# Row statistics made where the rows are finished, one square root per router head, and rows kept in on-chip memory between two stages of a four-layer block

## Chip, core and metric

The kernel runs on one core of a Trainium2 chip. The metric is the time of one execution on the device in microseconds (us), the median of the runs shown. All data is float32. TensorE is called PE, VectorE DVE, ScalarE ACT, GpSimd POOL; SyncE (SP) issues the DMA transfers that this change touches.

## The reference, cut to what matters

```
x = x + attention(layernorm(x))          # x is 2048 tokens by 512
x = x + ffn(layernorm(x))
x = x + rwkv(layernorm(x))               # recurrence over the 2048 tokens
x = x + ffn(layernorm(x))
layernorm(x) = (x - mean(x)) / sqrt(var(x) + 1e-5)      # over the 512 of a row
ffn(h): scores = sigmoid(h @ gate_w); 2 of 4 groups, 6 of 32 experts of each token
        sum of 6 weighted silu(h @ w_gate) * (h @ w_up) @ w_down
        + silu(h @ sw_gate) * (h @ sw_up) @ sw_down      # shared expert, 704 wide
```

## The kernel before

Tokens are 16 tiles of 128 rows, four tiles to a block, so there are four blocks (`NB = 4`, `BT = 4`). The stages run one after another: projections, attention, attention output (`stage_attn_out`), router with the shared expert (`stage_router`), experts (`stage_experts`), the recurrence (`stage_rwkv`), and router and experts again. Each stage is a block of programs, one for each engine, that are ordered among each other only by semaphores; a stage begins when all engines have ended the one before. Within an engine the order is the order written. Where precision asks for it a matrix is split into a high part (made by ACT) and a low part (made by DVE), and three products are added.

**Attention output.** For each of 16 tiles PE turns the heads, ACT makes the high part, DVE the low part (`low_heads`, L848), PE multiplies, and DVE adds the product to the residual rows `resid` (`add_rows`, L853). `resid` holds all 16 tiles in on-chip memory; the blocks lie in it in the order `ORDER = [2, 3, 0, 1]` (`place_of`).

**The router's head.** This is everything up to the first product of the shared expert, `up(0)` (L1613). In the second router SP first loads `resid` from DRAM, where the recurrence stored it (L1110). SP then loads the gate weights, the shared expert's up weights in two halves (`wup`, L1116) and its down weights (`wdown`, L1117 and L1119), then stores the normalized rows `xn` block by block (L1126). `xn` has room for two blocks: block 2 can be normalized only when block 0's store has landed (`xn_stored[0]`), block 3 when block 1's has.
- DVE: `statistics(0, 2, 1)` makes `bn_stats` (L1335) and `bn_aggr` (L1339) of eight tiles, adds epsilon, waits for ACT's square root, makes the reciprocal root in five short steps, and normalizes eight tiles (L144). Then `statistics(2, NB, 2)` does the same for the other eight, and `low_shared(0)` makes the low part of half the up weights.
- ACT: `root(0)`, the copies of blocks 0 and 1 after PE has turned them (`copy_block`, L1210, four copies a block), `copy_logits(0)` (L1216), `high_shared(0)` (L1248), `root(1)`, `copy_logits(1)`, `high_shared(1)`, `copy_block(2)`, `copy_block(3)`, `copy_logits(2)`, and the high part of block 2 (L1263). DVE makes its low part (L1365), and PE starts `up(0)`. The high part of the down weights (L1268) comes after that.
- PE: turns block 0, multiplies it with the gate, then block 1, then turns blocks 2 and 3 and multiplies both.

**The recurrence.** It runs over 16 units `n = 4 * b + c` (block `b`, quarter `c` of the channels). In each, PE makes three projections (24 products, L2375) and the output product of unit `n - 3` (eight products, L2387). DVE runs in this order: `sums(n-1)` (two scans, L2267 and L2269), `advance_peak(n)` (a scan, L2259, and a difference, L2262), `quotients(n-3)` (L2288), at `c == 3` `add_out(b-1)` (four additions of the output to `x_add`, L2302), `divide(n-2)` (three operations and a reciprocal, L2275 to L2280), `finish_mix` (L2254), at `c == 1` the row statistics of block `b + 2` (`stats`), at `c == 3` its normalization (`normalize`). POOL's four products of a unit (L2125, L2110, L2114, L2116) are released by `division_begun`, which DVE raises ahead of its reciprocal. After the last unit POOL does `fraction_top` of units 14 and 15 in one go. SP stores the sums of each block to DRAM (`time_mixed`, L2097), waits until the stores have landed, and loads `x_add` for the next block (L2101).

Of the kernel before, what the change touches and what calls it, by code (L numbers as in the profile page):

```python
# [31 lines left out]
BT = 4  # L32
# [65 lines left out]
class Norm:  # L98
# [5 lines left out]
    def __init__(self, k, name, scope, n_blocks=NB):  # L104
        nc = k.nc
        self.stats = scope.enter_context(nc.sbuf_tensor(f"{name}_stats", [P, n_blocks, BT, 6], F32))
# [708 lines left out]
def stage_attn_out(k, w, ident, heads, resid):  # L815

    nc = k.nc
    with ExitStack() as s:
# [10 lines left out]
        product, added = k.sem("c_product"), k.sem("c_added")  # L829

        k.clear_past()
        with nc.Block() as block:
# [12 lines left out]
            def _(v):  # L845
# [119 lines left out]
def stage_router(k, name, ident, resid, source, gate_w, shared_up, shared_down, xn_rows, acc_rows, disp, first, weights):  # L965
# [4 lines left out]
    with ExitStack() as s:  # L970
# [63 lines left out]
        norm = Norm(k, f"{name}_norm", s)  # L1034
# [41 lines left out]
        resid_loaded = [sem(f"resid_loaded{b}") for b in range(NB)]  # L1076
# [27 lines left out]
        with nc.Block() as block:  # L1104
            @block.sync
            def _(sp):
                if source is not None:
                    resid_in = rows(source)
                    for b in range(NB):
                        sp.dma_start(resid[:, place_of(b):place_of(b) + BT, :], resid_in[:, b * BT:(b + 1) * BT, :]).then_inc(resid_loaded[b], 16)  # L1110
                        if b == 0:
                            sp.dma_start(wg[:], gate_w).then_inc(gate_loaded, 16)
                else:
                    sp.dma_start(wg[:], gate_w).then_inc(gate_loaded, 16)
                for i in range(2):
                    sp.dma_start(wup[i][:], shared_up[:, :, UP_HALF[i]]).then_inc(up_loaded[i], 16)  # L1116
                sp.dma_start(wdown[:, 0:FULL, :], shared_down[0:FULL * P, :].rearrange("(c p) d -> p c d", p=P)).then_inc(down_loaded, 16)  # L1117
                for half in (slice(0, TAIL), slice(TAIL, P)):
                    sp.dma_start(wdown[half, FULL, :], shared_down[FULL * P:SM, :]).then_inc(down_loaded, 16)  # L1119
# [4 lines left out]
                for b in range(NB):  # L1124
                    sp.wait_ge(normed, (b + 1) * BT)
                    sp.dma_start(xn_out[:, b * BT:(b + 1) * BT, :], xn[:, b % 2 * BT:(b % 2 + 1) * BT, :]).then_inc(xn_stored[b % 2], 16)  # L1126
                for i in range(2):
# [76 lines left out]
            def _(act):  # L1204
# [36 lines left out]
                def root(n):  # L1241
                    span = slice(n * NB // 2, (n + 1) * NB // 2)
                    act.wait_ge(norm.var_ready, n + 1)
                    act.activation(norm.std[:, span, :], norm.var[:, span, :], ACT.Sqrt).then_inc(norm.std_ready, 1)

# [4 lines left out]
                root(0)  # L1250
# [4 lines left out]
                root(1)  # L1255
# [38 lines left out]
            def _(v):  # L1294
# [34 lines left out]
                def statistics(first, last, roots):  # L1329
                    span = slice(first, last)  # L1330
                    for b in range(first, last):
                        if source is not None:
                            v.wait_ge(resid_loaded[b], 16)
                        for t in range(BT):
                            chain.step(v.bn_stats(norm.stats[:, b, t, :], resid[:, place_of(b) + t, :]))  # L1335
                    chain.wait()
                    for b in range(first, last):
                        for t in range(BT):
                            chain.step(v.bn_aggr(norm.mean_var[:, b, t, :], norm.stats[:, b, t, :]))  # L1339
# [1185 lines left out]
```

## Time and profile before

| what | value |
|---|---|
| median of 3 runs | 3247.44 us (3246.61 to 3250.93) |
| profiled execution, its own time | 3245.94 us |
| its span | 3244.2 us |
| PE busy / DVE / ACT / POOL | 94% / 64% / 49% / 27% |
| attention output | ends at 849.94 us |
| first router and experts | 850.2 to about 1890 us |
| recurrence | about 1897 to 2182.47 us |
| second router and experts | 2185.05 us to the end |

A row of the time line has the start in us, the length in us, the engine, the line, the operation, what is written and read, the count of merged instructions, and in brackets how long the engine had idled and what released it. PEld is PE's loading of weights. In groups merged from several instructions the length reaches from the first start to the last end.

### The profile page before, as it was taken

Reading aid. Unit: us, or ns where it says so; the run is one execution under the profiler, and the core shown is the slowest. Engines: PE = TensorE matmul, PEld = TensorE weight load, DVE = VectorE, ACT = ScalarE, POOL = GpSimd, SP = SyncE. Lnnn points to the kernel's source line nnn. Section 1 sums busy time; section 2 is a strip of 40 time slices with the busy share of each in tenths; the row PEclk is TensorE's granted clock in tenths of the full one; section 3 lists DMA queues with packets and bytes.
Section 4 is the critical chain, followed back from the end, with each engine's and each line's share of the span. In section 5 each row is a group of like instructions: output and inputs, shape, how many; then the busy total and the mean of one; then the engine's idle time right before and its main releaser. Section 6 shows DMA issues by size and latency. Waiting matters only on the chain. (4 is left out here: it accounts for less than half of the span.)

```text
span 3244.2 us, 62788 instructions
## 1 busy us (share of the span) xinstructions
PE 3060.3 (94%) x15682; PEld 2414.2 (74%) x15683; DVE 2078.7 (64%) x3887; ACT 1591.8 (49%) x2096; POOL 867.9 (27%) x777
## 2 busy tenths in 40 slices
PE   8979999999799999999999969977999999999998
PEld 6745555555678799999999944436788999999997
DVE  5266666663686566666666659987765666666665
ACT  3224544444321366665665657634124666566665
POOL 0011000110011243333333313341113343333333
PEclk9969999999999999999999989998999999999999
DMA  6331111130300477776777540114016777777664
GB/s 188 113 77 41 41 40 40 40 105 1 125 30 29 129 180 170 177 176 165 183 180 174 115 147 0 52 52 176 30 48 174 187 186 177 171 181 170 169 153 77
DMA packets 142697, 378.72 MB, mean 117 GB/s; under 512 B 22144, under 2 KB 24960, under 8 KB 139008
## 3 DMA queue, kind: packets, MB, share of 16 engines
q1 hardware_dynamic: 88832, 248.20, 24.5%
q0 software_dynamic: 52608, 127.69, 20.8%
q10 hardware_dynamic: 1152, 1.57, 0.2%
q8 instruction: 48, 0.79, 0.1%
q14 instruction: 57, 0.47, 0.0%
HBM read 277.49 MB, written 99.91 MB: 116 GB/s over the span
## 5 line engine op out<-in xcount | busy, mean ns | idle before, releaser
L1905 DVE TENSOR_TENSOR first_lo<-first_raw,first_hi x230 | 557.8, 2425 | 95.3 <-ACT first_hi L1850 95.0
L1850 ACT ACTIVATE first_hi<-first_raw x230 | 465.4, 2023 | 23.0 <-DVE first_lo L1905 7.6
L607 ACT ACTIVATE b_probs<-b_p_cols 128x1024 f32<-128x1024 f32 (+1 forms) x320 | 269.2, 893 | 300.2 <-PE b_p_cols L739 299.1
L1898 DVE TENSOR_TENSOR g_hidden<-g_gate,g_p_up 128x352 f32<-128x352 f32 x232 | 120.9, 521 | 450.8 <-PE g_p_up L1965 447.1
L1861 ACT ACTIVATE g_y<-g_p_y,first_rows_in 128x512 f32<-128x512 f32 x232 | 160.0, 690 | 345.6 <-PE g_p_y L1981 345.5
L1963 PE MATMUL g_p_gate<-first_hi,first_rows_hi 128*128 (+1 forms) x928 | 319.1, 344 | 4.6 <-DVEq L1921 4.4
L638 DVE TENSOR_REDUCE b_part_max<-b_p_ring 128x1 f32<-128x512 f32 x384 | 246.4, 686 | 117.4 <-PE b_p_ring L724 115.2
L1802 POOL DMA_INDIRECT out_dram<-g_y,first_ids_out x116 | 186.4, 1607 | 441.7 <-ACT g_y L1861 327.8
L1802 POOL DMA_INDIRECT mixed_rows<-g_y,first_ids_out x116 | 183.9, 1585 | 443.4 <-ACT g_y L1861 331.1
L1964 PE MATMUL g_p_gate<-first_lo,first_rows_hi 128*128 (+1 forms) x928 | 300.5, 324 | 0.0
L1965 PE MATMUL g_p_gate<-first_hi,first_rows_lo 128*128 (+1 forms) x928 | 299.4, 323 | 0.0
L1965 PE MATMUL g_p_up<-first_hi,first_rows_lo 128*128 (+1 forms) x928 | 298.0, 321 | 0.0
L1963 PE MATMUL g_p_up<-first_hi,first_rows_hi 128*128 (+1 forms) x928 | 297.9, 321 | 0.0
L1964 PE MATMUL g_p_up<-first_lo,first_rows_hi 128*128 (+1 forms) x928 | 297.8, 321 | 0.0
L1979 PE MATMUL g_p_y<-first_hi,g_hidden_hi 128*128 (+2 forms) x696 | 275.3, 395 | 7.4 <-issue 5.6
L1980 PE MATMUL g_p_y<-first_lo,g_hidden_hi 128*128 (+2 forms) x696 | 274.5, 394 | 0.0
L1981 PE MATMUL g_p_y<-first_hi,g_hidden_lo 128*128 (+2 forms) x696 | 274.3, 394 | 0.0
L755 PE MATMUL b_p_out<-b_probs,b_v_pair 128*64 128x512 f32 (+3 forms) x1280 | 270.3, 543 | 0.0
L1791 POOL DMA_INDIRECT first_rows_in<-xn_rows,first_ids_in x232 | 241.6, 1042 | 71.7 <-issue 70.8
L724 PE MATMUL b_p_ring<-b_k_stack,b_q_stack 96*128 96x512 f32 (+3 forms) x640 | 220.4, 424 | 24.9 <-ACT b_shift_t L593 9.8
L1836 ACT ACTIVATE g_gate<-g_p_gate 128x352 f32<-128x352 f32 x232 | 108.1, 466 | 248.1 <-issue 188.1
L724 PEld LDWEIGHTS b_p_ring<-b_k_stack,b_q_stack 96*128 96x128 f32 x640 | 112.8, 197 | 149.9 <-issue 43.0
(364 smaller groups left out, 6473.8 us busy)
## 6 DMA issues: line engine op xcount, KB each, us to landing
first_raw<-in_expert_weights_dram SPq DMA_DIRECT2D x248, 544.0 KB, 8.0
qk_hi<-a_hi SPq DMA_DIRECT2D x32, 256.0 KB, 2.6
qk_lo<-a_lo SPq DMA_DIRECT2D x32, 256.0 KB, 2.9
xn_rows<-f_xn SPq DMA_DIRECT2D x8, 1024.0 KB, 8.3
b_q_stack<-qk_hi SPq DMA_DIRECT2D x28, 256.0 KB
b_k_stack<-qk_hi SPq DMA_DIRECT2D x28, 256.0 KB
first_raw<-in_expert_weights_dram SPq DMA_DIRECT2D x2, 2176.0 KB, 8.6
resid<-in_x_dram SPq DMA_DIRECT2D x4, 1024.0 KB, 10.8
```

Of the source, the lines that this page charges most:

```text
L607: act.activation(probs[:, q, :, 0:w], p_cols[:, m % NCOL, :, 0:w], ACT.Exp, scale=SCALE).then_inc(probs_ready, 1)
L724: pe.matmul(p_ring[:, ring, 0:w], q_stack[i][h][0:NPART, t * P:(t + 1) * P], k_stack[i][h][0:NPART, c * BW:c * BW + w], start=True, stop=T ...
L755: mm = pe.matmul(p_out[h * HV:(h + 1) * HV, d:BW], v_pair[i][:, kt, h, :], probs[:, m % NPROB, h, 0:BW - d], start=(kt == 0), stop=(m in l ...
L1802: pool.indirect_dma_start(out=acc_rows, out_offset=bass.IndirectOffsetOnAxis(ap=ids_out[:, i:i + 1].bitcast(U32), axis=0), in_=y[:, n, :], ...
L1850: act.activation(hi[:, bass.ds(place, PIECE)], raw[:, bass.ds(source, PIECE)], ACT.Copy).then_inc(split_hi_ready, 1)
L1905: v.tensor_tensor(lo[:, bass.ds(place, PIECE)], raw[:, bass.ds(source, PIECE)], hi[:, bass.ds(place, PIECE)].bitcast(F32), ALU.subtract).t ...
L1963: pe.matmul(p_g[:, i, 0:M], rows_hi[:, i, c, :], hi[:, columns], start=(c == 0), stop=False)
L1964: pe.matmul(p_g[:, i, 0:M], rows_hi[:, i, c, :], lo[:, columns], start=False, stop=False)
L1965: m = pe.matmul(p_g[:, i, 0:M], rows_lo[:, i, c, :], hi[:, columns], start=False, stop=(c == KD - 1))
L1979: pe.matmul(p_y[:, i, :], hidden_hi[0:z, i, c, :], hi[0:z, columns], start=(c == 0), stop=False)
L1980: pe.matmul(p_y[:, i, :], hidden_hi[0:z, i, c, :], lo[0:z, columns], start=False, stop=False)
L1981: m = pe.matmul(p_y[:, i, :], hidden_lo[0:z, i, c, :], hi[0:z, columns], start=False, stop=(c == MC - 1))
```

## The change

It has four parts.
1. `bn_stats` of a tile is made where the tile is finished: in the attention output after each `add_rows`; in the recurrence in four places, the last block's after each of its four additions, blocks 0, 1 and 2 at `n = 14, 15, 16` after `divide`. The results lie in one tensor, `row_stats`, that outlives the stages. Both routers read it.
2. The router's head aggregates all 16 tiles, takes one square root, and makes one reciprocal root for all.
3. The recurrence writes blocks 2 and 3 of its result straight to where the second router has `resid`. Blocks 0 and 1 still go through DRAM (`half_rows`) and are loaded to that place while the recurrence runs, after the third block's projections. The router loads nothing of `resid`.
4. SP loads the down weights behind the stores of `xn` blocks 0 and 1. In the recurrence `stats` and `normalize` stand ahead of `divide`, and POOL's last `fraction_top` waits for `division_begun` of its own unit.

```diff
 # stage_attn_out, DVE
                     v.tensor_tensor(resid[:, place, :], p_mm[:, t % 2, :], resid[:, place, :], ALU.add).then_inc(added, 1)
+                    v.wait_ge(added, t + 1)
+                    v.bn_stats(row_stats[:, t // BT, t % BT, :], resid[:, place, :]).then_inc(stats_ready, 1)
 # stage_router, SP
-                if source is not None:
-                    resid_in = rows(source)
-                    for b in range(NB):
-                        sp.dma_start(resid[:, place_of(b):place_of(b) + BT, :], ...).then_inc(resid_loaded[b], 16)
...
-                sp.dma_start(wdown[:, 0:FULL, :], ...).then_inc(down_loaded, 16)
-                for half in (slice(0, TAIL), slice(TAIL, P)):
-                    sp.dma_start(wdown[half, FULL, :], shared_down[FULL * P:SM, :]).then_inc(down_loaded, 16)
...
                 for b in range(NB):
                     sp.wait_ge(normed, (b + 1) * BT)
                     sp.dma_start(xn_out[:, b * BT:(b + 1) * BT, :], ...).then_inc(xn_stored[b % 2], 16)
+                    if b == 1:
+                        sp.dma_start(wdown[:, 0:FULL, :], ...).then_inc(down_loaded, 16)
+                        for half in (slice(0, TAIL), slice(TAIL, P)):
+                            sp.dma_start(wdown[half, FULL, :], ...).then_inc(down_loaded, 16)
 # stage_router, ACT
-                root(0)
+                act.wait_ge(norm.var_ready, 1)
+                act.activation(norm.std[:], norm.var[:], ACT.Sqrt).then_inc(norm.std_ready, 1)
                 copy_block(0)
                 copy_block(1)
                 copy_logits(0)
                 high_shared(0)
-                root(1)
                 copy_logits(1)
 # stage_router, DVE
-                statistics(0, 2, 1)
                 for b in range(NB):
-                    if b == 2:
-                        statistics(2, NB, 2)
+                    for t in range(BT):
+                        chain.step(v.bn_aggr(norm.mean_var[:, b, t, :], norm.stats[:, b, t, :]))
+                chain.wait()
+                v.tensor_scalar(norm.var[:], norm.mean_var[:, :, :, 1], EPS, None, ALU.add).then_inc(norm.var_ready, 1)
+                v.wait_ge(norm.std_ready, 1)
+...
+                for b in range(NB):
 # stage_rwkv, SP
-                for b in range(NB):
+                for b in range(NB - 1):
                     for t in range(BT):
                         sp.wait_ge(out_added, b * BT + t + 1)
-                        sp.dma_start(out_tiles[:, b * BT + t, :], x_add[:, t, :]).then_inc(out_stored[t], 16)
+                        if b < STORED:
+                            sp.dma_start(half_tiles[:, b * BT + t, :], x_add[:, t, :]).then_inc(out_stored[t], 16)
...
+                    if b == STORED - 1:
+                        sp.wait_ge(product, (NB - 1) * KD * 3)
+                        sp.wait_ge(mixed_ready, 3 * NB)
+                        for half in range(STORED):
+                            sp.dma_start(resid[:, place_of(half):place_of(half) + BT, :], half_tiles[...]).then_inc(resid_loaded, 16)
+                sp.wait_ge(resid_loaded, 16 * STORED)
 # stage_rwkv, POOL
-                pool.wait_ge(division_begun, UNITS - 1)
-                fraction_top(UNITS - 2)
-                fraction_top(UNITS - 1)
+                for n in range(UNITS - 2, UNITS):
+                    pool.wait_ge(division_begun, n + 1)
+                    fraction_top(n)
 # stage_rwkv, DVE
-                        v.tensor_tensor(x_add[:, t, :], p_out[:, t, :], x_add[:, t, :], ALU.add).then_inc(out_added, 1)
+                        into = x_add[:, t, :] if b < STORED else resid[:, place_of(b) + t, :]
+                        v.tensor_tensor(into, p_out[:, t, :], x_add[:, t, :], ALU.add).then_inc(out_added, 1)
+                        if b == NB - 1:
+                            v.wait_ge(out_added, b * BT + t + 1)
+                            v.bn_stats(row_stats[:, b, t, :], resid[:, place_of(b) + t, :]).then_inc(row_stats_ready, 1)
...
+                def row_statistics(b):
+                    if b < STORED:
+                        v.wait_ge(resid_loaded, 16 * STORED)
+                    for t in range(BT):
+                        v.bn_stats(row_stats[:, b, t, :], resid[:, place_of(b) + t, :]).then_inc(row_stats_ready, 1)
...
                     if c == 3 and 1 <= b < NB:
                         add_out(b - 1)
+                    if n < UNITS and b + 2 < NB and c == 1:
+                        stats(b + 2)
+                    if n < UNITS and b + 2 < NB and c == 3:
+                        normalize(b + 2)
                     if 2 <= n < UNITS + 2:
                         divide(n - 2)
+                    if UNITS - 2 <= n <= UNITS:
+                        row_statistics(n - (UNITS - 2))
                     if n < UNITS:
...
-                        if b + 2 < NB and c == 1:
-                            stats(b + 2)
-                        if b + 2 < NB and c == 3:
-                            normalize(b + 2)
```

## Rows read from the trace of the kernel before

**Rows 1.** Page, busy time by engine; busy time of the last expert stage.
```profile
PE 3060.3 (94%) x15682; PEld 2414.2 (74%) x15683; DVE 2078.7 (64%) x3887; ACT 1591.8 (49%) x2096; POOL 867.9 (27%) x777
...
2460.00:3244.00 784.00, 769.98 (x4591) 716.87 (x4588) 486.08 (x689) 466.20 (x577) 304.21 (x230) 0.99 0.69 164
```
**Rows 2.** Time line, end of the attention output.
```profile
841.18 0.69 DVE L848 TENSOR_TENSOR c_heads_lo<-c_p_turn,c_heads_hi 128x512 fp32r<-128x512 f32 x1 [0.38 <-ACT c_heads_hi L839]
...
842.90 0.59 PEld L868 LDWEIGHTS c_p_turn<-ident,heads 128*128 128x128 f32 x4
...
849.25 0.69 DVE L853 TENSOR_TENSOR resid<-c_p_mm,resid 128x512 f32<-128x512 f32 x1 [2.03 <-PE c_p_mm L881]
```
**Rows 3.** Time line, head of the first router.
```profile
850.22 1.28 ACT L1244 ACT_TABLE_LOAD   x1 [5.86 <-PEq L832]
850.26 4.84 DVE L1335 BATCH_NORM_STATS2 f_norm_stats<-resid 128x6 f32<-128x512 f32 x8 [0.32 <-PEq L832]
...
855.13 0.64 DVE L1339 BATCH_NORM_AGGREGATE f_norm_mean_var<-f_norm_stats 128x2 f32<-128x6 f32 x8
...
857.31 3.74 DVE L144 TENSOR_SCALAR f_xn<-resid,f_norm_mean_var,f_norm_rstd 128x512 f32<-128x512 f32 x8
...
871.00 2.38 ACT L1248 ACTIVATE f_wup_hi<-f_wup 128x2560 fp32r<-128x2560 f32 x1
...
874.87 0.60 ACT L1210 ACTIVATE f_xT_f<-f_p_down 128x512 f32<-128x512 f32 x1 [1.49 <-PE f_p_down L1561]
...
880.68 0.60 ACT L1216 ACTIVATE f_logits_t<-f_p_mm 128x512 f32<-128x512 f32 x1 [1.03 <-PE f_p_mm L1569]
...
884.38 0.50 PE L1613 MATMUL f_p_mm<-f_xT_hi,f_wup_hi 128*128 128x512 f32 x1 [1.90 <-DVE f_xT_lo L1365]
```
**Rows 4.** Time line, head of the second router; then its first products by tile.
```profile
2181.78 0.69 DVE L2302 TENSOR_TENSOR r_x_add<-r_p_out,r_x_add 128x512 f32<-128x512 f32 x1 [0.17 <-PE r_p_out L2387]
...
2190.85 2.47 DVE L1335 BATCH_NORM_STATS2 f_norm_stats<-resid 128x6 f32<-128x512 f32 x4 [8.38 <-DMA resid<-time_mixed]
...
2198.41 3.74 DVE L144 TENSOR_SCALAR f_xn<-resid,f_norm_mean_var,f_norm_rstd 128x512 f32<-128x512 f32 x8
...
2228.14 0.71 PE L1613 MATMUL f_p_mm<-f_xT_hi,f_wup_hi 128*128 128x512 f32 x1 [1.90 <-DVE f_xT_lo L1365]
...
L1613 PE MATMUL f_p_mm<-f_xT_hi,f_wup_hi x4: 392/628/713, 2228.1 to 2231.9; 128*128 128x512 f32 x4
```
**Rows 5.** Time line, ACT in the recurrence: a table load and the next root.
```profile
1961.65 1.28 ACT L131 ACT_TABLE_LOAD   x1
1962.94 0.21 ACT L131 ACTIVATE r_norm_std<-r_norm_var 128x4 f32<-128x4 f32 x1
```
**Rows 6.** DMA from 850 to 876 us: rate in 40 slices; stores' time to landing.
```profile
GB/s 0 8 93 126 175 369 411 416 425 403 410 421 390 406 399 381 391 384 381 334 315 309 331 378 394 394 400 397 397 394 394 183 16 0 0 0 0 66 372 388
...
xn_rows<-f_xn SPq DMA_DIRECT2D x4, 1024.0 KB, 8.3
```
**Rows 7.** Time line, the recurrence's middle: three DVE rows, then PE's.
```profile
2005.61 2.29 DVE L2254 TENSOR_TENSOR r_mixed<-r_mixed,r_shifted 128x2048 f32<-128x2048 f32 x1 [2.01 <-ACT r_shifted L2160]
...
2060.74 1.28 DVE L2259 TENSOR_TENSOR_SCAN r_state<-r_w,r_state,r_k 128x512 f32<-128x512 f32 x1 [1.43 <-ACT r_k L2167]
...
2087.36 2.28 DVE L2267 TENSOR_TENSOR_SCAN r_state<-r_kt,r_state 128x512 f32<-128x512 f32 x1
...
2043.54 0.79 PE L2363 MATMUL r_p_turn<-ident,r_xn 128*128 128x128 f32 x4 [5.02 <-DVE r_xn L144]
```
**Rows 8.** Time line, DVE at the recurrence's end.
```profile
2159.58 0.66 DVE L2288 TENSOR_TENSOR r_y<-r_top,r_below 128x512 f32<-128x512 f32 x1
...
2162.58 3.35 DVE L2280 RECIPROCAL r_below<-r_below 128x512 f32<-128x512 f32 x1 [0.16 <-DVE r_below L2278]
...
2166.31 1.68 DVE L2288 TENSOR_TENSOR r_y<-r_top,r_below 128x512 f32<-128x512 f32 x1 [0.38 <-POOL r_top L2116]
...
2175.60 0.69 DVE L2288 TENSOR_TENSOR r_y<-r_top,r_below 128x512 f32<-128x512 f32 x1
```

More of the change, by code:

```diff
@@ L812, in _, with stage_attn_out @@
                 turn_out(NPAIR - 1, NB - 1, bank("out", NSTEP))
-def stage_attn_out(k, w, ident, heads, resid):
+def stage_attn_out(k, w, ident, heads, resid, row_stats):
     nc = k.nc
@@ L962, in __init__, with stage_router @@
         self.release = sb("release", [1, E], I32)
-def stage_router(k, name, ident, resid, source, gate_w, shared_up, shared_down, xn_rows, acc_rows, disp, first, weights):
+def stage_router(k, name, ident, resid, row_stats, gate_w, shared_up, shared_down, xn_rows, acc_rows, disp, first, weights):
     nc = k.nc
@@ L1327, in tile_hots @@
                         v.tensor_scalar(row_hot[:, n % NR, :], iota_p[:], row_of[:, kk, t:t + 1], None, ALU.is_equal).then_inc(row_hot_ready, 1)
[L1329 to L1339, printed above, removed]
-                    chain.wait()
-                    v.tensor_scalar(norm.var[:, span, :], norm.mean_var[:, span, :, 1], EPS, None, ALU.add).then_inc(norm.var_ready, 1)
-                    v.wait_ge(norm.std_ready, roots)
-                    chain.link(v.reciprocal(norm.r0[:, span, :], norm.std[:, span, :]))
-                    chain.link(v.tensor_tensor(norm.half[:, span, :], norm.r0[:, span, :], norm.r0[:, span, :], ALU.mult))
-                    chain.link(v.tensor_tensor(norm.half[:, span, :], norm.half[:, span, :], norm.var[:, span, :], ALU.mult))
-                    chain.link(v.tensor_scalar(norm.half[:, span, :], norm.half[:, span, :], -0.5, 1.5, ALU.mult, ALU.add))
-                    chain.link(v.tensor_tensor(norm.rstd[:, span, :], norm.r0[:, span, :], norm.half[:, span, :], ALU.mult))
                 def low_shared(i):
@@ L2015, with stage_rwkv @@
 NEG = -1e38
-def stage_rwkv(k, ident, x_rows, mixes, decay, first, w_kvr, w_out, out_rows):
+def stage_rwkv(k, ident, x_rows, mixes, decay, first, w_kvr, w_out, half_rows, resid, row_stats):
     nc = k.nc
@@ L2069, in stage_rwkv @@
         x_add_loaded = [sem(f"x_add_loaded{t}") for t in range(BT)]
-        out_stored = [sem(f"out_stored{t}") for t in range(BT)]
-        x_tiles, out_tiles = rows(x_rows), rows(out_rows)
+        out_stored, resid_loaded, row_stats_ready = [sem(f"out_stored{t}") for t in range(BT)], sem("resid_loaded"), sem("row_stats_ready")
+        x_tiles, half_tiles = rows(x_rows), rows(half_rows)
+        STORED = NB // 2
+        assert sorted(ORDER[:STORED]) == list(range(STORED, NB))
         def shifted_of(b, j):
```

59 lines of the change are left out of this document (32 added, 27 removed).

## The prediction

> **What bounds the kernel now.** I read the page's busy times first. PE works 94% of the span, and the long expert stages are PE's alone: 770 of 784 us in the last one [rows 1]. Nothing in this change touches them. So the question is what the stretches cost in which PE waits: the two router heads and the recurrence. I went through these in order of time, engine by engine, and asked at each idle bracket what ended it. The reader is to see a relay in the heads. Statistics on DVE, a root on ACT, normalization, PE's turning, ACT's copies; none of it overlaps, and PE's first shared product comes only at its end. From the last addition of the attention output (849.25 + 0.69 = 849.94) to that product (884.38) it is 34.44 us; in the second head, from 2182.47 (2181.78 + 0.69) to 2228.14, it is 45.67 us [rows 2 to 4].
>
> **First head.** Five things change.
> - The tail of the attention output. DVE waits for PE before each addition (2.03 us before the last one), so 15 of 16 `bn_stats` go into idle time, at 4.84 / 8 = 0.61 us each [rows 2, 3]. Each pushes the next `low_heads` back by about 0.4 us; it ended at 841.87, and PE wanted it at 842.90, so 1.0 us of cover is left 0.6 [rows 2]. Without that cover it would be 0.4 us for each of 14 tiles, 5.6 us. The last `bn_stats` stands alone behind the last addition: +0.7.
> - From stage start (850.22) to the first normalization (857.31) it was 7.1 us. Now: 16 aggregations at 0.08, 1.3; from the last aggregation through the root to the normalization it was 857.31 - 855.77 = 1.54, and with twice the columns 1.6. That is 2.9 us: -4.2 [rows 3].
> - `root(1)` goes. It stood on ACT behind the first up half, so DVE could not normalize block 2 in time, and ACT, done at 873.38, idled 1.49 us until 874.87. With all rows normalized early it finds block 2 turned: -1.5 [rows 3].
> - ACT's eight copies of blocks 2 and 3 took 874.87 to 879.65 because PE turned blocks just ahead of them. At ACT's own pace, 0.5 each, about 4.1: -0.7. The wait of 1.03 ahead of `copy_logits(2)` shrinks to about 0.3, since PE turned block 3 ahead of ACT's last four copies: -0.7 [rows 3].
> Sum: 0.7 - 4.2 - 1.5 - 0.7 - 0.7 = -6.4.
>
> The down weights are needed only after `up(0)` begins, at 884 before and about 878 now, so their later load costs nothing if it lands by then. By order in SP's queue: gate and up weights 2.95 MB, spare rows 0.28, blocks 0 and 1 at 1.05 each, then 1.57 MB of down weights. The rate is about 0.40 MB per us, flowing some 3 us after the stage's start [rows 6]. Block 0's store lands about 10.7 us after that, 13.7 after the start; block 1's 2.6 later; the down weights 3.9 later still, at 20 us, and they are wanted at 27. Block 2 normalized then is turned by about 17, while ACT comes to it at about 19. So the slack of the stores is some 2 us, of the down weights 7.
>
> Is the table of the square root in time? Its load lasts 1.28 us from the stage's start, and the variance is now ready at 1.5 instead of 5.6 us [rows 3], so the cover shrinks to 0.2. The recurrence's rows have the root 0.01 us behind the load [rows 5]: nothing is added. The Trainium skill (ScalarE: Activation LUTs, What ACT_TABLE_LOAD costs) adds a drain of about 1.38 us to each switch of tables. By it the root would be 1.2 us late in each head and the time 2.4 us longer; this trace has no such gap behind the load, so I don't count it.
>
> **Second head.** It keeps the same instructions from its normalization on, so it takes what the first will: 2.9 to the first normalization and, from there, 27.07 - 1.5 - 0.7 - 0.7 = 24.2 to `up(0)`. Ahead of it stand the last `bn_stats` (0.7), about 0.3 for the stage to turn (849.94 to 850.22), and 0.5 because the `bn_stats` of tile 2 delays the addition of tile 3, which came 0.17 us after it was free to. That is 28.6 against 45.67: -17.1 [rows 3, 4]. Most of it is one thing: `resid` went to DRAM and back, DVE sat 8.38 us for it, and the stores of `xn` were queued behind 4.2 MB more [rows 4]. At the start of `up(0)` PE's products were slow (0.63 against 0.39 us) for 3.5 us, some 1.5 us lost; I leave that as it is, and keep -1.5 for the range [rows 4].
>
> **The recurrence, units 3 to 15.** `stats` and `normalize` move ahead of `divide` in three places that matter (units 3, 5, 7). Ahead of `divide` they run while POOL rests. Behind the reciprocal they shielded the scans: a scan took 2.28 us beside POOL and 1.28 without it [rows 7], so each move costs about 1 us, most of it given back by a small step of the normalization that POOL had held up. For: PE's turning no longer waits 5.02 us for the rows of block 3; DVE's wait of 1.43 for the projection two units later goes, and of the wait of 2.01 in unit 5 about 0.7 is won, since `stats` fills it [rows 7]. Together -0.7 in unit 5, +0.3 left of the contention in unit 7, -1.4 in unit 9: -1.8, which PE, busy without a gap from unit 12 to 15, carries to unit 15. I take -1.8; bounds are -5.0 (PE's whole wait) and +3.0 (three contended scans, no wait won).
>
> **Its end.** The 12 `bn_stats` of blocks 0 to 2 are 2.4 us for each of units 14, 15, 16. The first four are free: POOL ends meanwhile and both scans are uncontended. The second four displace two contended scans (they took 3.6 for 2.4): +1.2. The third four push `quotients(14)` from 2166.31 to 2169.5, +3.2 in all. Then POOL's later release pays back: from `quotients(14)` to the last reciprocal it was 5.90 us beside POOL, and without it the same steps took 3.00 (2159.58 to 2162.58), -2.9. Last, POOL's three products now begin with the reciprocal and end 3.65 us later, the reciprocal after 3.39, +0.3 [rows 8]. Together +0.65; with the units before: -1.2. `bn_stats` beside POOL is not in the trace. Its bounds are the reciprocal (3.35 us with POOL working) and a two-input operation (1.68 for 0.69) [rows 8]. It has one input like the reciprocal, so I take no slowing; the other end is +1 in each of three units. The Trainium skill (SBUF — State Buffer, Who interferes with whom) says that a DVE instruction with one input from on-chip memory does not contend with GpSimd. By that rule too the sum stays; by a lock for every instruction it would be 3 us more.
>
> The load of blocks 0 and 1 into `resid` is issued at about 2107 and needs some 7 us for 2.1 MB; DVE asks at about 2138. Hidden; were the cover gone, up to 7 us. Behind SP's two new waits stand only the loads for block 3's addition, wanted 25 us later.
>
> **Sum.** -6.4 - 17.1 - 1.2 = -24.7. The profiled execution took 3245.94 us and would take 3221.2; it stands 1.5 under the median of 3247.44, so I predict 3222.7 for the median.
>
> **Rivals.**
> 1. The stores become the bound. If the down weights share the queues with block 1's store instead of following it, it lands 3.9 us later, block 3 is turned 2 us after ACT wants it, in both heads: +4, 3226.7. For it: 2 us of slack is little. Against: before, landings agreed with the order of issue (8.3 us behind 4.6 MB of loads) [rows 6].
> 2. The recurrence gives back. All 12 `bn_stats` fully on the path (7.3), three contended scans (3.0), no wait won: +10.3 less POOL's 2.9, so +7.4 in place of -1.2: 3231.3. Against: DVE had idle time in units 5 and 9 [rows 7].
> 3. More is won. PE's 5.02 us come through whole (-3.2 more), and PE starts `up(0)` at full clock (-1.5): 3218.0.
> 4. Slower than before. PE rests about 25 us less, and its clock may be granted lower afterwards. The granted clock was 0.99 over the last expert stage [rows 1]; the two expert stages are about 1710 us. From a drop of 1.5% on it eats the whole gain; at 3% the time is 3274. Against: PE already works hundreds of microseconds on end there with no such drop.
> 5. The change does nothing. That needs a head bound by something that stays, such as ACT's copies; but ACT has nothing to copy before the first normalization, 13.4 us into the second head [rows 4].
>
> **How the numbers follow.** Forecast 0.62, rival 1 0.10, rival 2 0.14, rival 3 0.10, rival 4 0.03, rival 5 0.01. The range, 3215 to 3231, reaches from 3 us beyond rival 3 (the sum's many small gains may each be a little larger) to rival 2. A measurement can tell about 0.2% (6.5 us) from no change; so faster has 0.96, same 0.01, slower 0.03.
>
> **What would show it.** In the profile after: the first normalization 2.9 us after each router's start; no `resid` load; no idle of ACT between the second up half and block 2's copies; `up(0)` 27 us after each start; the last two reciprocals about 8.7 us apart, not 9.63. I would be wrong if DVE waits for `xn_stored` at block 2 after 16 us, or if scans beside POOL grow in number.

## The result and the profile after

The changed kernel took 3221.89 us (median of four), the kernel before 3247.03 in the same session. Three of the four executions took 3217.26 to 3223.50 us (median 3220.28) and one, far outside them, 12998.82; the ratio on record, 0.9913 with a 95% interval of 0.9898 to 0.9928, is estimated without it and is not the quotient of the two medians (0.9923). Forecast were 3222.7 and 3215 to 3231. The profiled execution took 3220.28 us, its span is 3218.2.

The page of the kernel after, its first lines and the granted clock in 40 slices, against [rows 1]:

```profile
span 3218.2 us, 62766 instructions
...
PE 3052.7 (95%) x15680; PEld 2411.1 (75%) x15683; DVE 2070.4 (64%) x3875; ACT 1588.8 (49%) x2094; POOL 871.4 (27%) x777
...
PEclk9969999999999999999999979999999999999999
```

PE's busy time is nearly the same (3052.7 us against 3060.3); what went is mostly time in which it waited. The span is 26.0 us shorter. Cut at the last additions and the first products of `up(0)`, from start to end of each stretch:

| stretch | before | after | difference | forecast |
|---|---|---|---|---|
| up to the last addition of the attention output | 849.94 | 846.41 | -3.5 | 0 |
| first head: that addition's end to `up(0)` | 34.44 | 29.22 | -5.2 | -6.4 |
| `up(0)` to the recurrence's first instruction | 1012.9 | 1021.0 | +8.1 | 0 |
| recurrence, to the end of its last addition | 285.2 | 283.2 | -2.0 | -1.2 |
| second head | 45.67 | 28.10 | -17.6 | -17.1 |
| second `up(0)` to the end | 1016.1 | 1010.3 | -5.7 | 0 |

The three changed stretches give -24.8 where -24.7 was forecast. The three others moved by -3.5, +8.1 and -5.7 and nearly cancel. None of this can be put down to the change: the first stretch ends anywhere from 845.57 to 849.60 us in the executions of the experiments, and the last section comes back to the expert stages.

The timeline of the kernel after, first head, against [rows 3]:

```profile
847.42 1.28 ACT L1241 ACT_TABLE_LOAD   x1 [6.57 <-PEq L832]
849.24 0.21 ACT L1241 ACTIVATE f_norm_std<-f_norm_var 128x16 f32<-128x16 f32 x1 [0.53 <-DVE f_norm_var L1327]
850.80 3.87 DVE L144 TENSOR_SCALAR f_xn<-resid,f_norm_mean_var,f_norm_rstd 128x512 f32<-128x512 f32 x8
...
862.35 1.92 DVE L144 TENSOR_SCALAR f_xn<-resid,f_norm_mean_var,f_norm_rstd 128x512 f32<-128x512 f32 x4 [7.69 <-DMA xn_rows<-f_xn]
...
865.01 2.38 ACT L1238 ACTIVATE f_wup_hi<-f_wup 128x2560 fp32r<-128x2560 f32 x1
867.24 0.64 ACT L1205 ACTIVATE f_xT_f<-f_p_down 128x512 f32<-128x512 f32 x1
...
871.93 0.60 ACT L1211 ACTIVATE f_logits_t<-f_p_mm 128x512 f32<-128x512 f32 x1 [0.63 <-PE f_p_mm L1547]
...
875.63 0.79 PE L1591 MATMUL f_p_mm<-f_xT_hi,f_wup_hi 128*128 128x512 f32 x1 [1.90 <-DVE f_xT_lo L1343]
```

The middle part of the relay is gone. There is one root for 16 columns instead of two, normalization begins 3.4 us after the start, and ACT goes from the second up half (865.01) into block 2's copies without a bracket. DVE has a new wait: 7.69 us until block 0's store has landed, at 862.35, 14.9 us after the start. The row alone doesn't say whether it costs anything; experiment e1 is about that.

The second head, against [rows 4]:

```profile
2179.09 0.67 DVE L2290 TENSOR_TENSOR time_mixed<-r_p_out,r_x_add 128x512 f32<-128x512 f32 x1
2180.78 1.28 ACT L1241 ACT_TABLE_LOAD   x1 [30.68 <-PEq L2057]
...
2182.23 0.22 ACT L1241 ACTIVATE f_norm_std<-f_norm_var 128x16 f32<-128x16 f32 x1 [0.16 <-DVE f_norm_var L1327]
2183.64 3.81 DVE L144 TENSOR_SCALAR f_xn<-time_mixed,f_norm_mean_var,f_norm_rstd 128x512 f32<-128x512 f32 x8
2195.60 1.92 DVE L144 TENSOR_SCALAR f_xn<-time_mixed,f_norm_mean_var,f_norm_rstd 128x512 f32<-128x512 f32 x4 [8.15 <-DMA xn_rows<-f_xn]
...
2207.86 0.50 PE L1591 MATMUL f_p_mm<-f_xT_hi,f_wup_hi 128*128 128x512 f32 x1 [1.90 <-DVE f_xT_lo L1343]
```

Normalization comes 2.86 us after the start (13.36 before), `up(0)` 27.08 after it. DVE's wait for block 0's store, 8.15 us here, was 1.65 before. The root begins 0.17 us after the table load's end (2180.78 + 1.28 = 2182.06), released by the variance.

The recurrence: the first scans of units 1 and 15, the third group of row statistics, and the last quotients, against [rows 7, 8]:

```profile
1936.24 1.28 DVE L2246 TENSOR_TENSOR_SCAN r_state<-r_w,r_state,r_k 128x512 f32<-128x512 f32 x1 [3.29 <-ACT r_k L2154]
...
2142.35 1.28 DVE L2246 TENSOR_TENSOR_SCAN r_state<-r_w,r_state,r_k 128x512 f32<-128x512 f32 x1
...
2163.92 2.41 DVE L2299 BATCH_NORM_STATS2 row_stats<-time_mixed 128x6 f32<-128x512 f32 x4
...
2173.15 0.69 DVE L2275 TENSOR_TENSOR r_y<-r_top,r_below 128x512 f32<-128x512 f32 x1 [0.54 <-POOL r_top L2103]
```

Between those scans lie 206.11 us; before it was 207.85 (1937.51 to 2145.36). So the middle gave 1.74. PE's waits for the rows of blocks 2 and 3 (1.88 and 5.02 us before) are gone. From unit 15's scan to `quotients(15)` it is 30.80 against 30.24, +0.56. Two of the signs named ahead can be read here. The last two reciprocals are 8.60 us apart (8.7 forecast, 9.63 before). Scans slowed beside POOL did grow in number among the sums of units 0 to 13, from 13 to 16: one scan each of units 3, 5 and 7 took 2.28 us and not 1.28. The prediction's sum had counted this as the price of the new order, so this sign did not separate right from wrong. The four scans of units 14 and 15 took 1.54 to 2.22 us before and 1.27 after.

### The profile page after: what moved, and what is told of

It reads as the page before. It is cut to its first block and busy times, and to the rows that moved or that the text cites. A ratio compares the mean times of both kernels' runs of the same rounds, so it can differ in the third digit from the quotient of the medians.

```text
span 3218.2 us, 62766 instructions
## 1 busy us (share of the span) xinstructions
PE 3052.7 (95%) x15680; PEld 2411.1 (75%) x15683; DVE 2070.4 (64%) x3875; ACT 1588.8 (49%) x2094; POOL 871.4 (27%) x777
```

## Experiments

Twelve runs in three groups (e0 to e3, e4 to e7, e8 to e11), each group on one chip with its own runs of the kernel before (3247.47, 3249.10 and 3248.39 us). The changed kernel's own median was 3221.89, 3214.74 and 3218.20 us in different groups, so each experiment is read by the stretches of its profiled execution, and the median stands beside them. Ratios are against the kernel before. "Head" is always from the end of the last addition to the start of `up(0)`.

**The yardstick, twice: e0 and e11.** The changed kernel unaltered, in the first and in the third group.

> The changed kernel itself, unaltered, as the yardstick for the others of this group. Expected 3221.9 us (3218 to 3225), 0.991 of the kernel before. In the profile: first normalization 3 us after each router's start, up(0) 27 to 28 us after it.

> The changed kernel once more, unaltered, on the same chip as these three: 3214 to 3222 us; the stretches from each router's start to up(0) as before, 27.1 to 28.6 us; the expert stages differ by up to 10 us from one execution to the next, which is what the medians can't tell apart.

3214.74 us (0.9894, 0.9879 to 0.9909) and 3218.20 us (0.9902, 0.9882 to 0.9921). Heads 29.54 and 28.60 in e0, 29.12 and 29.15 in e11.

**The down weights ahead of the stores: e1.**

```
+                sp.dma_start(wdown ...)            # ahead of the stores
                 for b in range(NB):
                     sp.dma_start(xn_out[b] ...)
-                    if b == 1:
-                        sp.dma_start(wdown ...)
```

> The down weights are issued before the stores of xn again (1.57 MB ahead of block 0's store, some 3.9 us at 0.40 MB per us); everything else is as in the changed kernel. Theory (the stores are the next bound, with 2 us of slack at most): block 0's store lands about 18.7 us after the router's start and not 14.9, DVE's wait for it at block 2 grows from 8 to 12 us, ACT and PE then wait some 2 us for block 2's rows, and up(0) comes 1.5 to 3 us later in each head, together +3 to +6 us against the changed kernel. Rival (the stores are hidden anyway, since ACT has its copies and the up weights to do): 0, with up(0) still 27 to 28 us after the start.

3222.52 us (0.9922, 0.9908 to 0.9935), +7.8 against e0. Heads 32.78 and 34.01: +3.2 and +5.4. The timeline of its second head:

```profile
2187.58 1.91 DVE L144 TENSOR_SCALAR f_xn<-time_mixed,f_norm_mean_var,f_norm_rstd 128x512 f32<-128x512 f32 x4 [12.37 <-DMA xn_rows<-f_xn]
...
2189.55 1.12 PE L1538 MATMUL f_p_down<-ident,f_xn 128*128 128x128 f32 x4 [5.78 <-DVE f_xn L144]
...
2201.55 0.51 PE L1590 MATMUL f_p_mm<-f_xT_hi,f_wup_hi 128*128 128x512 f32 x1 [1.90 <-DVE f_xT_lo L1342]
```

Block 0's store lands 19.0 us after the start, 3.8 later than in e0, and `up(0)` follows it in full; in the first head it lands 3.7 later and `up(0)` comes 3.2 later. In the second head PE rested 5.78 us before block 2 and then turned at the lower clock (1.12 for four, 0.66 in e0): the 1.6 us more of this head. The transfer was not hidden. With the rest of the change in place, the later load of the down weights is worth about 8 us, and the slack of 2 us that I gave the stores is 0.5 in the first head and none in the second.

**The round trip through DRAM again: e2.**

```
+                        sp.dma_start(half_tiles[b, t], resid[place_of(b) + t])    # recurrence, blocks 2 and 3
+                for b in range(NB):                                               # router, SP
+                    sp.dma_start(resid[b] <- half_rows[b]).then_inc(again_loaded[b], 16)
+                    v.wait_ge(again_loaded[b], 16)                                # router, DVE, ahead of block b
```

> The recurrence stores all four blocks of its output to DRAM again, waits for the last stores before it ends, and the second router loads all 4.2 MB back and waits for each block ahead of its normalization; the row statistics stay where the changed kernel makes them (in place of the loaded rows the same values were in on-chip memory, so this adds transfers and no arithmetic). Theory (most of the second head's 17 us was the transfer, not the statistics): the drain of the last stores gives +2 to +2.5 us, the first normalization comes some 9 us after the start and not 2.9 since block 0 has to land, the stores of xn stand behind 4.2 MB more and block 2 waits for them: up(0) some 10 to 14 us later in the second head, nothing in the first; together +10 to +15. Rival (the gain was the statistics and the single root): at most +2 to +4, by the drain alone, with up(0) 27 to 30 us after the start.

3228.63 us (0.9936, 0.9922 to 0.9949), +13.9; second head 40.10, +11.5; first head 29.50, unchanged. Its second head:

```profile
2182.01 1.91 DVE L144 TENSOR_SCALAR f_xn<-time_mixed,f_norm_mean_var,f_norm_rstd 128x512 f32<-128x512 f32 x4 [2.88 <-DMA time_mixed<-half_rows]
...
2200.95 1.92 DVE L144 TENSOR_SCALAR f_xn<-time_mixed,f_norm_mean_var,f_norm_rstd 128x512 f32<-128x512 f32 x4 [14.21 <-DMA xn_rows<-f_xn]
...
2213.86 0.50 PE L1598 MATMUL f_p_mm<-f_xT_hi,f_wup_hi 128*128 128x512 f32 x1 [1.90 <-DVE f_xT_lo L1350]
```

DVE waits only 2.88 us for the rows themselves. The larger price is the queue: the stores of `xn` stand behind 4.2 MB more, block 2 comes 24.65 us after the start, 9.4 later than in e0, and 1.5 us go to the drain before the stage can turn. So with everything else in place the round trip costs the second head 11.5 us. Such prices don't add up to the gain: in the second head the down weights (5.4, e1), the round trip (11.5) and the statistics (8.3, e3, below) make 25.2 us where the whole change gave 17.6, and in the first head e1 and e3 make 12.5 us for 5.2. Each delay, put back alone, costs what the others would partly have hidden.

**The statistics in the head: e3.** All 16 `bn_stats` at the head of each router, none in the attention output or the recurrence.

```
-                    v.bn_stats(row_stats[...], resid[:, place, :])      # attention output
-                        if b == NB - 1: ... v.bn_stats(...)             # recurrence, last additions
-                    if UNITS - 2 <= n <= UNITS: row_statistics(...)     # recurrence
+                        chain.step(v.bn_stats(norm.stats[:, b, t, :], resid[:, place_of(b) + t, :]))   # router
```

> All 16 statistics of rows are made at the head of each router again, the single root kept; none in the attention output or the recurrence. Theory (DVE's idle time in the attention output and POOL's late release covered them): first head +9 less the 0.7 of the last one's tail, since the first normalization comes 16 x 0.61 = 9.8 us later; second head the same; the recurrence's end gets back some 3 us, the price of the eight statistics on its path. Together +11 to +15 us. Rival (the statistics cost the same wherever they stand): 0 to +3.

3231.58 us (0.9941, 0.9928 to 0.9955), +16.8; heads 38.87 and 36.85, +9.3 and +8.3. Its second head begins, and its recurrence ends, so:

```profile
2170.28 0.69 DVE L2277 TENSOR_TENSOR r_y<-r_top,r_below 128x512 f32<-128x512 f32 x1 [0.55 <-POOL r_top L2105]
...
2175.78 9.59 DVE L1323 BATCH_NORM_STATS2 row_stats<-time_mixed 128x6 f32<-128x512 f32 x16 [0.32 <-PEq L2059]
```

`quotients(15)` stands 27.85 us behind unit 15's first scan, where e0 has 30.80 and the kernel before 30.24. So at the recurrence's end the statistics cost 2.9 us ahead of it and 1.4 us more up to the last addition (the additions are 1.31 us apart and not 0.86), against 9.6 us for all 16 in the head. By stretches the sum is 9.3 + 8.3 - 4.4 = 13.2, within the 11 to 15 expected. The profiled execution also has a second expert stage 10 us longer than e0's, which no statistic reaches.

**Divide first: e4.**

```
-                    if n < UNITS and b + 2 < NB and c == 1: stats(b + 2)
-                    if n < UNITS and b + 2 < NB and c == 3: normalize(b + 2)
                     divide(n - 2)
...
                             finish_mix(b + 1, c - 1)
+                        if b + 2 < NB and c == 1: stats(b + 2)
+                        if b + 2 < NB and c == 3: normalize(b + 2)
```

> In the recurrence, the statistics and the normalization of a block stand behind the division of the unit again, as in the kernel before; all else is as in the changed kernel. Theory (my sum of the recurrence's middle): DVE's wait of 1.43 and PE's of 5 us for block 3's rows come back, the scan behind the normalization is uncontended again; unit 15 begins 1.8 us later, so +1.8 us (bounds -3 to +5). Rival (the order is worth nothing, the 1.74 us came from another part of the change): 0, or below.

3218.99 us (0.9907, 0.9891 to 0.9923). Two of its waits in the recurrence from 1960 to 2060 us (total, times, longest), and the two scans:

```profile
PE r_p_turn L2362 <- DVE r_xn L144: 6.9, 2, 5.0
...
DVE r_mixed L2241 <- ACT r_shifted L2147: 4.0, 2, 2.0
```
```profile
1924.49 1.28 DVE L2246 TENSOR_TENSOR_SCAN r_state<-r_w,r_state,r_k 128x512 f32<-128x512 f32 x1 [1.60 <-ACT r_k L2154]
...
2132.61 1.28 DVE L2246 TENSOR_TENSOR_SCAN r_state<-r_w,r_state,r_k 128x512 f32<-128x512 f32 x1 [0.41 <-ACT r_k L2154]
```

208.12 us between the scans; every other kernel with the new order has 206.0 to 206.1. PE's wait of 5.0 for block 3's rows is back, the slowed scans of units 0 to 13 are 13 again and not 16, and 2.0 us are lost. So the order is the cause of the middle's gain, and the waits that it takes away outweigh the three slowed scans.

**POOL's last product early: e5.** `fraction_top(15)` released by unit 14's division, as before.

```
-                for n in range(UNITS - 2, UNITS): pool.wait_ge(division_begun, n + 1); fraction_top(n)
+                pool.wait_ge(division_begun, UNITS - 1); fraction_top(UNITS - 2); fraction_top(UNITS - 1)
```

> POOL's product for unit 15 is released by unit 14's division again and not by its own. Theory: POOL then works beside the quotients of unit 14 and the last reciprocal's run-up, so the steps from those quotients to the last reciprocal take up to 2.9 us more (5.9 for 3.0), less 0.5 for the product that no longer ends last: +1 to +2.4 us in the recurrence's end, the low end if the third group of row statistics, which stands between, covers part of POOL's time. Rival (what slows DVE there is its own length, not POOL): -0.5, the wait for the product gone and nothing lost.

3215.39 us (0.9898, 0.9882 to 0.9913). `quotients(15)` comes 31.58 us behind unit 15's scan, +0.78, under the 1 to 2.4 us expected. DVE and POOL there:

```profile
2153.81 2.41 DVE L2299 BATCH_NORM_STATS2 row_stats<-time_mixed 128x6 f32<-128x512 f32 x4
2156.13 1.03 DVE L2275 TENSOR_TENSOR r_y<-r_top,r_below 128x512 f32<-128x512 f32 x1
2157.19 1.64 DVE L2262 TENSOR_TENSOR r_below<-r_e,r_state 128x512 f32<-128x512 f32 x1
...
2154.13 1.26 POOL L2097 TENSOR_TENSOR r_v<-r_e,r_v 128x512 f32<-128x512 f32 x1
```

Two operations with two inputs are slowed (1.03 for 0.67, 1.64 for 0.69), then POOL is done, because the four `bn_stats` had covered most of its time; they take 2.41 us beside POOL and POOL takes its usual 1.26 beside them. In this kernel the late release is worth 0.8 us, not 2.6.

**Three statistics for each tile: e6.** Work is added here: two more `bn_stats` of each tile in the attention output, into memory that nothing reads.

```
                     v.bn_stats(row_stats[...], resid[:, place, :])
+                    for again in range(2): v.bn_stats(extra[:, t, again, :], resid[:, place, :])
```

> Adds work: the attention output makes each tile's row statistics three times, twice of them into memory that nobody reads. Theory (0.6 us of cover are left for low_heads after one statistic): two more, 1.2 us, overrun it by about 0.6 us in each of 14 tiles, 8 us, and 1.2 us more stand behind the last addition: +9 us. Rival (DVE's idle time of 2 us ahead of each addition takes all of it, and low_heads is asked for later than I read): +1.2 us, the tail alone.

3216.45 us (0.9894, 0.9878 to 0.9910). The rival holds, and not the 9 us of the theory: from the first to the last addition it is 47.90 us against 47.51 in e0, +0.4. The router starts 1.2 us later behind the last addition, but even this does not show in the head's length in this execution (29.52 against 29.54). Its timeline, then e0's at the same place:

```profile
840.47 0.67 DVE L849 TENSOR_TENSOR c_heads_lo<-c_p_turn,c_heads_hi 128x512 fp32r<-128x512 f32 x1
...
841.28 0.48 PE L884 MATMUL c_p_mm<-c_w_hi,c_heads_hi 128*128 128x512 f32 x1
...
844.38 0.50 PE L884 MATMUL c_p_mm<-c_w_hi,c_heads_hi 128*128 128x512 f32 x1
```
```profile
840.12 0.67 DVE L848 TENSOR_TENSOR c_heads_lo<-c_p_turn,c_heads_hi 128x512 fp32r<-128x512 f32 x1
...
842.15 0.47 PE L881 MATMUL c_p_mm<-c_w_hi,c_heads_hi 128*128 128x512 f32 x1
```

What waits for `low_heads` is the product behind PE's next turn. In e0 it starts 1.36 us after `low_heads` ends (840.79 to 842.15), in e6 0.14 us (841.14 to 841.28). I had compared with the turn itself, which asks for an older tile.

**Filling two gaps on DVE: e7.**

```
                 low_shared(0)
+                low_shared(1)
...
-                low_shared(1)
...
-                    if UNITS - 2 <= n <= UNITS: row_statistics(n - (UNITS - 2))
+                    if UNITS - 2 <= n < UNITS: row_statistics(n - (UNITS - 2))
+                    if n == UNITS + 1: row_statistics(2, range(2))     # behind divide(15)
+                    if n == UNITS + 2: row_statistics(2, range(2, BT)) # behind quotients(15)
```

> Two orders on DVE changed, no work added: in the routers low_shared(1) stands ahead of the low halves of the first tokens, in DVE's idle time before the last turned block, and in the recurrence the third group of row statistics is split, two tiles behind the last division and two behind the last quotients, where POOL's product is waited for. Theory (PE waits 5.3 us in each router behind up(0) for DVE's chain of the routing, and low_shared(1), 2.8 us, is part of that chain): -2.8 us in the first router, -1.9 in the second, -1.7 at the recurrence's end: -6 us against the changed kernel. Rival (up(0) comes later by what the chain gains, since the low halves stand behind low_shared(1)): -1.7 from the recurrence alone.

3218.46 us (0.9900, 0.9883 to 0.9916): a miss in both halves. Its timeline and two of its waits (total, times, longest):

```profile
873.27 2.49 DVE L1344 TENSOR_TENSOR f_xT_lo<-f_xT_f,f_xT_hi 128x512 fp32r<-128x512 f32 x4
878.67 3.36 DVE L1346 TENSOR_TENSOR f_wdown_lo<-f_wdown,f_wdown_hi 128x3072 fp32r<-128x3072 f32 x1 [2.91 <-ACT f_wdown_hi L1258]
...
2164.86 5.40 PE L2390 MATMUL r_p_out<-r_wo,r_y 128*128 128x512 f32 x8 [3.72 <-DVE r_y L2275]
```
```profile
PE f_p_down L1622 <- DVE f_acc L1309: 5.3, 1, 5.3
```

In the router the gap only moved: `low_shared(1)` had filled the time in which ACT makes `wdown_hi`, and now DVE waits 2.91 us there. In the second router PE's wait of 5.3 us stands 46.96 us behind `up(0)` as in e0, and has the same length: moving `low_shared(1)` did not shorten what it waits for. In the recurrence `quotients(15)` did come 1.3 us earlier, but PE, rested for 3.72 us and not 3.2, made its last products in 5.40 us where the profile after has 3.70.

**What the stores leave: e8, e9 and e10.** ACT now seemed the bound of the head (in e0 it works without a bracket from 861.98 to 873.8), and by e1 the stores were one too. e9 moves ACT's work alone, e8 the loads with it, e10 adds e7's split of the statistics.

```
-                for i in range(2): sp.dma_start(wup[i] ...)          # e8: wup[0] here, wup[1] behind block 1's store
                 copy_logits(1)
-                high_shared(1)
...
                 copy_logits(3)
+                high_shared(1)                                       # e8 and e9
```

> A new order in both routers, no work added: the second half of the up weights is loaded behind block 1's store of xn (and the down weights behind it), and ACT makes its high half behind the high halves of the first tokens instead of ahead of block 2's copies. Theory (ACT's own work bounds the head from block 1's copies to up(0), and the stores have little slack, so both must move together): the stores land 3.3 us earlier (1.31 MB at 0.40 MB per us), up(0) starts 2.38 us earlier in each head, at about 26.1 and 25.2 us after the start, together -4 to -4.8 us. Rival (the gain is given back behind up(0): low_shared(1) and the down weights' halves end 2.1 us later against up(0), and the routing on DVE behind them): up(0) earlier, but the product that waits 5.3 us for acc comes 48.5 and 47.0 us after up(0) no longer but up to 2 us later, net 0 to -1.

> Only ACT's order of the kernel before this one in the list: the high half of the second up weights behind the first tokens' high halves; the loads stay in the changed kernel's order. Theory (the stores now bound block 3): up(0) 1.3 to 1.8 us earlier in each head, since block 3 is normalized 2.5 us behind block 2's rows and turned only then; -2.6 to -3.6 in all, 1 to 2 less than with the loads moved too. Rival (the stores have their slack still): -2.38 in each head, as much as with the loads moved.

> The second up half late in both routers, and the recurrence's third group of row statistics split in two pairs, behind the last division and behind the last quotients. Candidate for a faster version. Expected: what the late half gives, -4 to -4.8, and -0.6 from the split (the last quotients 1.3 us earlier, PE's last products at the half clock as in the run with the split, +0.7): -4.6 to -5.4 us against the changed kernel. Rival: the two add to nothing measurable, since an expert stage that waits once for a late load moves the time by as much.

e9: 3213.62 us (0.9891, 0.9873 to 0.9910), heads 29.71 and 28.23: nothing, where 1.3 to 1.8 us in each were expected. e8: 3210.64 us (0.9879, 0.9860 to 0.9898), heads 26.67 and 26.72: -2.9 and -1.9 against e0. e10: 3209.53 us (0.9879, 0.9859 to 0.9900), heads 27.26 and 26.16. Second heads, e9 and then e8:

```profile
2184.44 1.91 DVE L144 TENSOR_SCALAR f_xn<-time_mixed,f_norm_mean_var,f_norm_rstd 128x512 f32<-128x512 f32 x4 [8.20 <-DMA xn_rows<-f_xn]
...
2187.10 0.60 ACT L1205 ACTIVATE f_xT_f<-f_p_down 128x512 f32<-128x512 f32 x1 [0.81 <-PE f_p_down L1539]
...
2189.94 0.60 ACT L1205 ACTIVATE f_xT_f<-f_p_down 128x512 f32<-128x512 f32 x1 [0.77 <-PE f_p_down L1539]
...
2196.78 0.80 PE L1591 MATMUL f_p_mm<-f_xT_hi,f_wup_hi 128*128 128x512 f32 x1 [1.90 <-DVE f_xT_lo L1343]
```
```profile
2190.82 1.91 DVE L144 TENSOR_SCALAR f_xn<-time_mixed,f_norm_mean_var,f_norm_rstd 128x512 f32<-128x512 f32 x4 [4.69 <-DMA xn_rows<-f_xn]
...
2196.76 0.65 ACT L1205 ACTIVATE f_xT_f<-f_p_down 128x512 f32<-128x512 f32 x1
...
2205.16 0.50 PE L1591 MATMUL f_p_mm<-f_xT_hi,f_wup_hi 128*128 128x512 f32 x1 [1.90 <-DVE f_xT_lo L1343]
```

In e9 ACT comes early and waits for block 2 and block 3; from block 2's normalization to `up(0)` are 12.34 us, exactly as in e0. In e8 the store lands 11.4 us after the start, ACT finds block 2 turned, and the head is shorter. So ACT's order alone gives 0, and with the loads moved too it gives 2 to 3 us. That the stores and ACT are two bounds of about equal length fits this; the loads moved alone were not run. A little is given back: PE's 5.3 us wait comes 47.3 us after `up(0)` where the changed kernel, at the same granted clock of 1.00, has 46.96. e8 and e10 are clearly faster than the kernel before; against the changed kernel the heads show about -5, of which some 0.7 is given back, and the medians -7.6 and -8.7 beside e11. But the intervals overlap, so the size of that gain stays open. In e10 the split did as in e7: `quotients(15)` 1.3 us earlier, PE's last products in 5.40 us.

## Why the prediction was right, step by step

- **Tail of the attention output.** +0.7 as said (the last `bn_stats` took 0.69). The cover of `low_heads` was 1.36 us and not 0.6 (e6); the term of zero was right for a better reason than mine.
- **Normalization.** Forecast 2.9 after the start; 2.86 in the second head, 3.38 in the first, where single small operations took longer (0.36 for 0.22). Behind the table load the root waited only for its variance, until 0.54 and 0.17 us after the load's end. The Trainium skill (ScalarE: Activation LUTs, What ACT_TABLE_LOAD costs) adds 1.38 us to a switch of tables; they don't show here.
- **`root(1)`, the copies, `copy_logits`.** The sum is as forecast in the second head (27.08 after the start, forecast 27.1), though the wait ahead of `copy_logits(2)` is 0.63 and not 0.3. The first took 28.21: 0.5 from the normalization, the rest from PE's gate products at the lower clock, for which block 1's first copy waited 2.22 us. That is the mis-sized term: -5.2 for -6.4.
- **Stores and down weights.** This step failed, though the sum did not show it. I put block 0's landing at 13.7 and its slack at 2 us; it landed at 14.8 to 15.2 and the slack was 0 to 0.5 (e1). Rival 1 put 4 us in both heads together on a delay of 3.9; e1 measured 3.2 + 5.4 for 3.8, twice as much. That the forecast held in spite of it is luck in part: the landing came about where it begins to cost.
- **Second head.** -17.6 for -17.1. The 28.6 that I forecast held 0.5 us for the delayed addition of tile 3, which lies ahead of this stretch; without it the sum gives the 28.1 measured. I called most of the gain one thing, the round trip; e2 prices it at 11.5, with everything else in place, and mostly as the queue ahead of the stores and not as the 8.38 us that DVE sat.
- **Units 3 to 15.** -1.74 for -1.8; e4 returns 2.0. The three slowed scans that the sum counted are the ones seen. How the rest divides among the waits was not tested.
- **The recurrence's end.** +0.56 for +0.65 up to `quotients(15)`. In the profile after the parts hold too: `quotients(14)` +2.95 against unit 15's scan (3.2 forecast), from there to the last reciprocal 3.01 us for 5.90 (-2.9), from that to `quotients(15)` +0.5 (0.3 forecast). As a price of the late release, though, 2.9 is too much: it is worth 2.4 us, net, without the statistics (e3 against before) but 0.8 with them (e5), since they cover POOL's work as well. And between the last additions the `bn_stats` cost 1.4 us and not 0.5. In the profile after PE made those last products in 3.70 us and not 5.40 and hid this (0.26 us less than before from `quotients(15)` to the last addition). The stretch's other 0.56 us went ahead of unit 1's scan, for which I have no cause. In e11 PE took 6.48 and `quotients(15)` to the last addition 7.6 us instead of 5.9.
- **`bn_stats` beside POOL** took 2.41 us for four (e5), the same as without it (9.59 for 16 in e3). By these rows the rule that the prediction took from the Trainium skill (SBUF — State Buffer, Who interferes with whom), that a DVE instruction with one input from on-chip memory does not contend with GpSimd, holds here. The page says it for instructions outside DVE's two-port modes.
- **The median.** That it fell within a us of the forecast is partly luck: the other stages happened to cancel, and e0 and e11 gave 3214.7 and 3218.2.

## What to carry to other kernels

When a wait for a transfer is in the way, look at what the transfer's place in the queue delays as well: here the stores behind it cost more than the load itself. A slack that is worked out from two estimates of landing and arrival should be tried by delaying the transfer once, since a second bound of about equal length can hide the gain of a single move. Delays put back one at a time give prices that overlap, so they are not shares of the gain. Statistics of a row are cheap where the row is made and DVE waits anyway (0.6 us each, hidden, in the attention output); at the busy end of the recurrence they cost 4.4 us together, and gathered in the head 9.6.

## What the runs showed of the hardware

- **The granted clock after short rests.** The recurrence's last eight products took 3.70 us at the full level (2.4 GHz), and 5.40 or 6.5 to 6.7 us partly or wholly at the lower one (1.2 GHz). Behind a rest of PE of 0.7 to 1.8 us (e0, e1, e4, e5, e9) it was 3.70 each time; behind 3.23 us it was 3.70 twice (the profile after, e3) and 6.5 to 6.7 four times (e2, e6, e8, e11); behind 3.72 (e7, e10) and 4.61 (before) it was 5.40. What decides behind 3.23 us stays open. The same holds for `up(0)`: in the changed kernel's order PE's next wait comes 46.96 us behind it where the granted clock of that stretch is 1.00, 48.3 to 49.1 where it is 0.96 to 0.97 (e0, e3, e6, e11 and the profile after), and 49.8 where it is 0.93 (the second head of e6, the first of e7).
- **A late load in the expert stage.** The 14 profiled executions have 28 stretches of router and experts, from an `up(0)` to the recurrence or to the end. In all of them ACT waits 6.9 to 8.7 us for weights once, early in the stage. In six of them one expert's weights come late in mid-stage too: ACT waits 5.9 to 7.8 us for them and PE 3.1 to 4.9 us behind ACT. These six took 1017.7 to 1021.0 us (the first stretch of the profile after and of e8; the second of e3, e4, e7 and e8), the other 22 took 1008.7 to 1016.7. PE's wait is not all of it: in the 12 us around it the granted clock was 0.72 in e7, and 1.00 at the same place in e0. So the +8.1 us of the result's first stretch is such a load, and the -5.7 of the second (1016.1 and 1010.3 us) is a difference without one.

```profile
ACT first_hi L1828 <- DMA first_raw<-in_expert_weights_dram: 11.1, 5, 7.5
...
PE g_p_y L1957 <- DVE g_hidden_lo L1888: 5.4, 2, 4.7
```

These are waits of e7 from 2250 us on: total, times, longest. With stretches that differ by up to 12 us between executions, changes of 2 us can't be told from medians of four to seven executions, and can from the stretches that the change touches.
